# Post-norm state-space block on one core: in pass B every second tile is turned by the DMA queue from f16 halves instead of by TensorE, and its chain runs two tiles further ahead

## What is computed

```python
xn = (x - mu) / jnp.sqrt(var + LN_EPS) * ln_gamma + ln_beta
delta = sigmoid(xn @ w_delta + b_delta); B_t = xn @ w_in + b_in; gate = sigmoid(xn @ w_gate + b_gate)
h_t = tanh((h_{t-1} * delta_t) @ A + B_t)              # 2048 steps, 16 states
x = layernorm(x + (hs @ C) * gate + x)
x = layernorm(x + real(ifft(fft(x) @ w)) + bias)
```

## Time and profile before

| | |
|---|---|
| median of 3 runs | 868.49 us (868.31 to 868.72) |
| profiled execution | 867.59 us, its span 865.7 us |
| granted TensorE clock, mean | 0.997 |
| busy: PE, DVE, ACT, POOL | 842.7, 720.1, 588.1, 588.5 us |
| pass A alone | 0 to about 400 us |
| pass B alone | from about 430 us |
| DMA | 209.52 MB, mean 242 GB/s |

### The profile page before, as it was taken

How to read it: one execution, slowest core, us unless ns; L and a number is a source line. 1 busy time by engine, 2 the same in 40 slices (tenths; PEclk the granted TensorE clock), 3 DMA queues, 4 the chain that set the end, 5 groups by cost and what they waited for, 6 DMA issues and landing times.

```text
span 865.7 us, 16633 instructions
## 1 busy us (share of the span) xinstructions
PE 842.7 (97%) x5062; PEld 453.1 (52%) x5094; DVE 720.1 (83%) x1432; ACT 588.1 (68%) x1183; POOL 588.5 (68%) x938
## 2 busy tenths in 40 slices
PE   8899999999999999999999999999999999999996
PEld 6445454554555555555455555545555555555553
DVE  7888777889989888897689898899788888888883
ACT  4355445745655445555578888898788888888887
POOL 3576666798765646676666676767677777777672
PEclk9999999999999999999999999999999999999998
DMA  8389899777767668678365756577876766776743
GB/s 315 146 300 322 317 311 318 256 277 258 260 226 246 199 239 296 240 247 290 122 219 185 230 190 240 201 250 240 262 237 237 258 232 238 257 242 236 250 146 145
DMA packets 94189, 209.52 MB, mean 242 GB/s; under 512 B 3760, under 2 KB 5040, under 8 KB 90160
## 3 DMA queue, kind: packets, MB, share of 16 engines
q1 hardware_dynamic: 93840, 208.49, 69.7%
q10 hardware_dynamic: 288, 0.27, 0.2%
HBM read 139.53 MB, written 67.11 MB: 239 GB/s over the span
## 4 chain that ended last, share of the span: by engine, by line
PE 84%; DVE 6%; issue 3%; ACT 2%; DMA 2%; POOL 1%; another core or an unknown queue 0%; DVEq 0%; POOLq 0%; ACTq 0%
PE bank L1522 23%; PE bank L1525 22%; PE bank L1523 22%; PE bank L1493 6%; PE bank L1605 3%; PE bank L1678 3%; DMA x_sb<-x 2%; PE bank L1555 1%; PE bank L1585 1%; DVE bn L1265 1%; PE bank L1558 1%; DVE gsum_sb L1312 1%; DVE xs_sb L1297 1%; PE bank L1473 1%; POOL x_sb L921 0%
## 5 line engine op out<-in xcount | busy, mean ns | idle before, releaser
L826 POOL TENSOR_TENSOR lo_sb<-xs_sb,hi_sb 128x512 f16<-128x512 f32 x128 | 149.3, 1167 | 116.1 <-ACT hi_sb L562 115.8
L921 POOL TENSOR_TENSOR x_sb<-x_sb,gate_sb 128x512 f32<-128x512 f32 x120 | 153.4, 1279 | 70.2 <-DMA x_sb<-x 63.1
L1522 PE MATMUL bank<-wg_hi,hi_sb 128*128 128x512 f16 x508 | 192.6, 379 | 6.9 <-DVE gsum_sb L1312 2.8
L1522 PE MATMUL bank<-w_re_sb,hi_sb 128*128 128x512 f16 x512 | 194.0, 379 | 1.2 <-DVE w_ring L1396 0.7
L1523 PE MATMUL bank<-w_re_sb,hi_sb 128*128 128x512 f16 x512 | 194.0, 379 | 0.0
L1523 PE MATMUL bank<-wg_lo,hi_sb 128*128 128x512 f16 x508 | 192.3, 378 | 0.0
L562 ACT ACTIVATE hi_sb<-xs_sb 128x512 f16<-128x512 f32 x128 | 80.3, 628 | 125.3 <-DVE xs_sb L1297 125.0
L1302 DVE SCALAR_TENSOR_TENSOR lo_sb<-bank,hi_sb 128x512 f16<-128x512 f32 x128 | 88.5, 692 | 57.1 <-ACT hi_sb L747 55.7
L1525 PE MATMUL bank<-w_re_sb,lo_sb 128*128 128x512 f16 x512 | 131.4, 379 | 0.0
L1525 PE MATMUL bank<-wg_hi,lo_sb 128*128 128x512 f16 x508 | 130.4, 379 | 0.0
L755 ACT ACTIVATE norm_sb<-x_sb,lift_bias,rstd 128x512 f32<-128x512 f32 x128 | 103.2, 806 | 15.0 <-POOL lift_bias L934 14.6
(11 more groups left out here) (197 smaller groups left out, 1378.7 us busy)
## 6 DMA issues: line engine op xcount, KB each, us to landing
x_sb<-x SPq DMA_DIRECT2D x63, 1024.0 KB, 6.3
gate_dram<-gate_sb SPq DMA_DIRECT2D x32, 1024.0 KB, 5.3
out<-out_sb SPq DMA_DIRECT2D x31, 1024.0 KB, 5.4
gate_sb<-gate_dram SPq DMA_DIRECT2D x30, 1024.0 KB, 7.0
out_sb<-x_turned SPq DMA_DIRECT2D x16, 1024.0 KB, 7.4
norm_sb<-x_turned SPq DMA_DIRECT2D x15, 1024.0 KB, 7.3
w_ring<-gate_dram SPq DMA_DIRECT2D x2, 1024.0 KB, 9.5
x_sb<-x SPq DMA_DIRECT2D x2, 512.0 KB, 6.1
```

The lines of the kernel that those rows point to most:

```text
L826: pool.tensor_tensor(lo_sb[:, k % 4], xs_sb[:, k % 2], hi_sb[:, k % 4], ALU.subtract).then_inc(s_lo, 1)
L921: pool.tensor_tensor(x_sb[:, k // 4, k % 4], x_sb[:, k // 4, k % 4], gate_tile(n, k), ALU.add).then_inc(s_v, 1)
L1522: nc.tensor.matmul(dst, hi_sb[:, slot_of, t], w_hi[:, t], start=(t == 0), stop=False)
```

## The change

Tiles with an odd number are no longer transposed by TensorE. ACT writes the f16 high half of the normalised tile as it lies, rows on partitions (`flat_high`), DVE the low half (`flat_low`), both into a view of `wp_rep` that holds two tiles; SP turns each half with one transposing DMA of 128 x 512 f16 (`turn`), into the same `hi_sb` and `lo_sb` that `ffn` reads. Even tiles stay as they were, with four buffers of `hi_sb` and `lo_sb` in use and not two. Around it:

- `states_out`, `gated`, `residual`, statistics, factors and `b_normalise` run two slots earlier (n + 9, n + 8, n + 7, n + 6, n + 5, n + 4); `norm_sb` grows to eight tiles with `w_im_sb`. The flat halves of odd tile n + 3 are written in slot n.
- x is loaded in halves of two tiles (`load_x_half`), each asked for as soon as its two tiles are normalised; between them stand the two transposes of an odd tile.
- the gates of octet 1 are loaded into `out_sb`; at the end of pass A the order of SP is written anew (`end_of_first_pass`), and the last gate store of pass A stands behind `second_pass(0, 0)`.
- SP's octets 7 to 14 are written out and no loop.

```diff
+        flat_halves = wp_rep[:].rearrange("p a t b c s -> p (a t b c s)").bitcast(F16).rearrange(
+            "p (i h d) -> p i h d", i=2, h=2)
...
+            def turn(n, k, v):
+
+                i = k // 2 % 2
+                if before(n, 4):
+                    sp.wait_ge(s_f, n - 3)
+                else:
+                    sp.wait_ge(s_proj, TILES - 3 + n)
+                sp.wait_ge(s_flat_hi, v * 4 + k // 2 + 1)
+                sp.dma_start(hi_sb[:, k % 4], flat_halves[:, i, 0], transpose=True).then_inc(s_turned[i], 16)
+                sp.wait_ge(s_flat_lo, v * 4 + k // 2 + 1)
+                sp.dma_start(lo_sb[:, k % 4], flat_halves[:, i, 1], transpose=True).then_inc(s_turned[i], 16)
...
             def second_pass(v, q):
                 if before(v, 1):
+                    if isinstance(v, int) and v == 1:
+                        sp.wait_ge(s_gst[q], 16 * OCTETS)
                     sp.wait_ge(s_v, v * 8 + 4 * q + 4)
                     load_gate(v + 1, q)
-                elif q == 1:
-                    sp.wait_ge(s_gst[1], 16 * OCTETS)
-                    load_gate(1, 1)
+                for half in range(2):
+                    sp.wait_ge(s_bnorm, v * 8 + 4 * q + 2 * half + 2)
+                    load_x_half(v + 1, q, half)
+                    k = 4 * q + 2 * half + 1
+                    turn(v * 8 + k, k, v)
                 if before(v, 1):
                     store_result(v - 1, q)
-                sp.wait_ge(s_bnorm, v * 8 + 4 * q + 4)
-                load_x(v + 1, q, s_bx)
...
+            def flat_high(n, k, v):
+                act.wait_ge(s_bnorm, n + 1)
+                if before(n, 4):
+                    act.wait_ge(s_turned[k // 2 % 2], (v * 2 + k // 4) * 32)
+                nc.scalar.activation(flat_halves[:, k // 2 % 2, 0], norm_tile(k), ACT.Copy,
+                                     scale=ROW_SCALE).then_inc(s_flat_hi, 1)
...
+            def flat_low(n, k, v):
+                dve.wait_ge(s_flat_hi, v * 4 + k // 2 + 1)
+                if before(n, 4):
+                    dve.wait_ge(s_turned[k // 2 % 2], (v * 2 + k // 4) * 32)
+                nc.vector.scalar_tensor_tensor(flat_halves[:, k // 2 % 2, 1], norm_tile(k), ROW_SCALE,
+                                               flat_halves[:, k // 2 % 2, 0], ALU.mult,
+                                               ALU.subtract).then_inc(s_flat_lo, 1)
...
-            def ffn(n, k):
-                pe.wait_ge(s_bhi, n + 1)
-                pe.wait_ge(s_blo, n + 1)
+            def ffn(n, k, v):
+                if k % 2:
+                    pe.wait_ge(s_turned[k // 2 % 2], (v * 2 + k // 4) * 32 + 32)
+                else:
+                    pe.wait_ge(s_bhi, v * 4 + k // 2 + 1)
+                    pe.wait_ge(s_blo, v * 4 + k // 2 + 1)
...
             def slot_b(n, k, v):
                 scan_slot(1, n)
-                if exists(n + 1):
-                    transpose(n + 1, k + 1, s_bnorm, s_bhi, s_blo, s_bt)
-                if exists(n + 7):
-                    states_out(n + 7, (k + 7) % 8, v if k < 1 else v + 1)
+                if k % 2 == 1 and exists(n + 1):
+                    transpose(n + 1, (k + 1) % 8, v + (k + 1) // 8)
...
                 if exists(n):
-                    ffn(n, k)
+                    ffn(n, k, v)
```

More of the change, by code:

```diff
@@ L276, in gate_tile @@
                 return w_ring[:, k]
+            if isinstance(n, int) and n < 16:
+                return out_sb[:, k // 4, k % 4]
             return gate_sb[:, k // 4, k % 4]
@@ L384, in build @@
         s_last = sem("b_last_stored")
-        s_bx = [sem(f"b_x_loaded{i}") for i in range(2)]
+        s_bx = [[sem(f"b_x_loaded{i}_{half}") for half in range(2)] for i in range(2)]
+        s_flat_hi = sem("b_flat_high")
+        s_flat_lo = sem("b_flat_low")
+        s_turned = [sem(f"b_turned{i}") for i in range(2)]
         s_bg = [sem(f"b_gate_loaded{i}") for i in range(2)]
@@ L461, in load_gate, with load_x_half @@
             def load_gate(v, q):
-                sp.dma_start(gate_sb[:, q], gate_v[v, q]).then_inc(s_bg[q], 16)
+                dst = out_sb[:, q] if isinstance(v, int) and v == 1 else gate_sb[:, q]
+                sp.dma_start(dst, gate_v[v, q]).then_inc(s_bg[q], 16)
+            def load_x_half(v, q, half):
+                two = slice(2 * half, 2 * half + 2)
+                sp.dma_start(x_sb[:, q, two], x_v[v, q][:, two]).then_inc(s_bx[q][half], 16)
+            def turn(n, k, v):
[8 more added lines that the diff above has]
+                sp.dma_start(lo_sb[:, k % 4], flat_halves[:, i, 1], transpose=True).then_inc(s_turned[i], 16)
             def replicate_states(g, odd):
@@ L470, in replicate_states, with end_of_first_pass @@
                                  src[first:first + 32]).then_inc(s_hrep[g][odd], 16)
-            for v in range(OCTETS):
+            def end_of_first_pass():
+                sp.wait_ge(s_xs, TILES - 12)
+                load_turned(OCTETS - 1, 0)
+                sp.wait_ge(s_bn, TILES - 4)
+                for half in range(2):
+                    load_x_half(0, 0, half)
+                sp.wait_ge(s_gsig, TILES - 12)
+                sp.dma_start(gate_v[OCTETS - 2, 0], gate_sb[:, 0]).then_inc(s_gst[0], 16)
+                sp.wait_ge(s_xs, TILES - 8)
+                load_turned(OCTETS - 1, 1)
+                sp.wait_ge(s_bn, TILES)
+                for half in range(2):
+                    load_x_half(0, 1, half)
+                sp.wait_ge(s_gsig, TILES - 8)
+                sp.dma_start(gate_v[OCTETS - 2, 1], gate_sb[:, 1]).then_inc(s_gst[1], 16)
+                sp.wait_ge(s_msplit, 4)
+                load_gate(1, 0)
+                first_pass(OCTETS - 1, 0)
+                sp.wait_ge(s_xs, TILES)
+                load_gate(1, 1)
+            for v in range(OCTETS - 2):
                 first_pass(v, 0)
@@ L476, in _ @@
                     replicate_states(0, 0)
[L477 to L486, removed]
+                first_pass(v, 1)
                 if v == 1:
@@ L525, in _ @@
             second_pass(6, 1)
-            with sp.Fori(7, OCTETS - 1) as v:
+            for v in range(7, OCTETS - 1):
                 second_pass(v, 0)
                 second_pass(v, 1)
[L529 to L532, removed]
+            for q in range(2):
+                for half in range(2):
+                    k = 4 * q + 2 * half + 1
+                    turn(TILES - 8 + k, k, OCTETS - 1)
+                store_result(OCTETS - 2, q)
+            store_result(OCTETS - 1, 0)
             for b in range(4):
```

113 lines of the change are left out of this document (63 added, 50 removed).

## The result

| | before | after |
|---|---|---|
| median | 868.61 us (868.31 to 869.72, 4 runs) | 857.68 us (856.57 to 858.25, 4 runs) |
| span of the profiled execution | 865.7 us | 855.8 us |
| granted TensorE clock | 0.997 | 0.996 |

The ratio is 0.987 [0.9853, 0.9887]: 10.9 us faster, where 23 were forecast (845.5 us). The sign was right, and 857.68 lies in the range of 838 to 925, but outside the likeliest case's own range of 838 to 852.

A forecast was written before the change was run, and what follows sets the result against it. TensorE was taken as the bound, busy 842.7 of 865.7 us. Terms 28.2 - 2.2 - 0.6 - 2 = 23.4 us off 867.6 gave 844.2, stated as a median of 845.5 us; range 838 to 925 us.

The forecast's parts named there:

- likeliest case: Whole kernel: the forecast itself holds, with a time of 838 to 852 us; chance 0.44.
- TensorE, 28.2 us: Pass B on TensorE: 64 tiles lose four transposes each, 0.44 us a tile, 28.2 us gained, all on the path.
- DVE's wait for POOL: Steady part: an odd tile's two-SBUF-input low half waits for POOL's residual, 0.25 us each, 5.7 us a pair, under TensorE's 6.04.
- DVE's wait for POOL locks in: Rival, steady part: every odd low half waits 1.2 us, 6.64 us a pair, about 872 us; halfway 858; 852 to 866: 0.12.
- The state split: Stretch 562 to 596 us: DVE limits a pair to 6.5 us of 6.8, gaining 0.3 not 0.44; 0.6 us taken back.
- The uneven meeting, 2 us: Steady part: 2 us taken off the gain for engines at 94% busy that meet unevenly.
- Beside the scan: Pass B during the scan: DVE needs 7.07 us a pair against TensorE's 6.92, becomes the bound, takes back 2.2 us.
- The DMA price, 0.7 us: SP's DMA queue: each of 128 transposing copies takes 0.7 us, which fits beside the other traffic at no cost.
- upper bound of 3.3 us: DMA queue: a transpose cut into 256 B runs, each costing a present packet's 103 ns, takes 3.3 us; whole kernel 1153 us.
- The doubt that got 0.24 of the chances: Rival, SP's queue: transposes fill the DMA engines, gain gone at 1.08 us each; up to 925 us 0.18, beyond 0.06.
- The signs of being wrong: TensorE waiting for DMA-written hi_sb or lo_sb, DMA share near 1, SP transpose issue over 1 us, odd low-half mean above 1.2.
- slack of 6.5: Transposed halves on SP's queue: they may land up to 6.5 us after issue before landing decides the time.

The follow-up runs named there:

- e2: Against the changed kernel: DVE's low half of odd tiles left out, both transposes turn the high half, gate product ahead of the statistics' aggregate; 852.03 us, ratio 0.9831 to before.
- e4: Against the changed kernel: POOL's residual works on 64 of 512 columns, so the result is incomplete; 846.73 us, ratio 0.9759 to before.
- e3: Against the changed kernel: the 128 transposing DMAs left out, odd tiles multiplied with old data; 853.88 us, ratio 0.9847 to before.
- e7: Against the changed kernel: a third, unused transposing DMA of 128 x 512 added to 60 odd tiles; 874.37 us, ratio 1.0082 to before.
- e6: Against the changed kernel: TensorE transposes every tile again, the two-slot lead, x halves and SP's order stay; 866.34 us, ratio 0.9994 to before.

## Why the prediction came out as it did

- **TensorE, 28.2 us**: right. Where little else binds, pairs take 6.05 us (e2) for 6.04, and beside the scan 3.70 + 3.22 = 6.92 us (e4) for 6.92.
- **The step that failed: DVE's wait for POOL, "I take 0.25 us for each odd tile: 5.7 us a pair, under TensorE's 6.04".** In the steady part the wait is 0.64 us, and 0.22 more are idle before it: 6.3 us a pair, above 6.04. The mechanism and its source row were right and the size was not. The 0.2 us were a mean over 16 starts at other positions; here POOL's residual starts at nearly the same place of each DVE slot that has a flat low half (0.27 to 0.57 us before it, all 24 times). The "for" of the rival "DVE's wait for POOL locks in" was visible: DVE's order is fixed, and the row of `h_lo` showed it 0.34 us into a residual. I gave the band around its halfway figure 0.12. That this figure, 858, is what came (857.68) is partly luck: it counted the wait in the steady part, and only 3.7 of the missing 13.6 us lie there.
- The Trainium skill ("SBUF — State Buffer", SBUF: two separate sides) says the same as the rows: a VectorE operation with two SBUF inputs and a GpSimd operation that reads SBUF exclude each other, and the first to start holds the ports for its whole duration. The trace agrees: 0.69 us becomes 1.52, ending behind the residual, and 0.72 with a residual of 320 ns.
- **The state split, "a gain of 0.3"**: wrong in sign, 7.72 us a pair for 6.9 before. I added the wait of the low half and not that the existing two-input operation, `h_lo`, would be held more often in the new order (811 ns for 595). e4 shows it: 25.5 and 13.2 us, the forecast of both rows.
- **"The uneven meeting, 2 us"** had no place for the stretch where the states are copied, 3.7 us over its forecast. 2.9 us go with the transposing DMAs (e3) and 0.8 with the long residual (e4). I looked for a DMA limit in a steady four tiles, not in the burst behind SP's wait for the split.
- **Beside the scan**: 7.07 us a pair forecast, 3.69 + 3.33 = 7.02 measured. The number is right and its parts are not: the low half waits 0.03 us there, not 0.25, and line 1181's operation (line 1236 now) has 705 ns, for 654.
- **The DMA price, 0.7 us**: by the queue's time 1.0, and 0.7 for the third one in e7. The upper bound of 3.3 us was far off: the packets of 256 B came as it assumed, but took 25 ns and not 103. The doubt that got 0.24 of the chances was not what decided, but SP's queue has little left: one transpose more for each odd tile turns the gain into a loss (e7).
- **The sum's last line**: 844.2 and 0.9 make 845.1 us, not 845.5. Nothing hangs on it.
- **The signs of being wrong**: all four came. A mean of the low half above 1.2 us (1.33) was the one that counted. TensorE waited for `lo_sb` twice, 2.3 us in all. A DMA share near 1 and SP issuing a transpose for over 1 us came too, and neither binds in the steady part (e2, e4).
- The Trainium skill ("Advanced Engine Details and Errata", X-Bar Transpose) has transposes as fast as plain copies. By the queue's time the trace does not agree: 131 kB in 1.0 us of all engines are 131 GB/s, while four tiles' plain traffic ran at 342. This is the price in a mix of transfers; what a transpose reaches alone no run shows.
- **Landing**: the medians, 4.6 and 3.7 us, were under the slack of 6.5, but from 650 to 800 us 12 of 24 high halves and 3 of 24 low ones landed later than that, up to 8.2 us, and TensorE did not wait for them there. So the slack was counted too small. **Lead**: nothing by itself in all, right (e6). **SP's issue**: 1.2 to 2.6 us for a transpose, not the 0.6 assumed for the slack; hidden in the steady part, where SP issues for 65% of the time, and not in the burst.

## What to carry to other kernels

Before an operand in PSUM is replaced by one in SBUF, lay the VectorE operation beside the GpSimd operations in time: if both stand at fixed places of one slot, the wait between them is either nothing or much the same in every slot, and a mean over other meetings is no price for it. Count it also for the two-input operations that were there already. And check a DMA budget in the stretch where the issuing engine has just been held by a wait, not only in the steady part; add up the issuing engine's own time in it, too.
